# A post-norm attention and int8 FFN layer on one core: rows of the maxima first on SyncE, a wait before stacking queries, and a new table of places

## The reference

```python
q = (x @ Wq) ; k = (x @ Wk) ; v = (x @ Wv)          # heads of 32; k, v shared by 4 query heads
attn = softmax(q @ k.T / sqrt(32)) ; o = (attn @ v) @ Wo
x = layernorm(x + o)
x_scale = max(|x|, axis=2) / 127 ; x_q = round(x / x_scale)
y = (x_q @ w_q.T) * x_scale * w_scale + bias
x = layernorm(x + y)
```

## Time and profile before

| what | value |
|---|---|
| median of 3 runs | 813.49 us (812.19 to 815.58) |
| the profiled execution | 815.75 us, span 813.5 us |
| PE busy | 741.5 us (91%) |
| DVE, POOL, ACT busy | 622.9, 590.9, 479.7 us |
| mean granted TensorE clock | 0.963 |

### The profile page before, as it was taken

The page is one execution under the profiler, slowest core; times in us unless marked ns, Lnnn a source line. Parts: engine busy times, 40 slices in busy tenths (PEclk is TensorE's granted clock), DMA queues, the critical chain, the costliest instruction groups (busy, mean ns, idle before and its releaser), DMA issues.

```text
span 813.5 us, 12175 instructions
## 1 busy us (share of the span) xinstructions
PE 741.5 (91%) x3640; PEld 435.0 (53%) x3640; DVE 622.9 (77%) x1103; ACT 479.7 (59%) x872; POOL 590.9 (73%) x700
## 2 busy tenths in 40 slices
PE   6689989999899989999899998999899998998874
PEld 5355545666366644566446663666446673544431
DVE  5678777778887787877878788877878787888365
ACT  3145556656665565665656566665666566666734
POOL 3208858786987589774988679874988759889825
PEclk9989999999999999999999999999999998999995
DMA  7431313234242323223232332323332342022101
GB/s 216 116 115 43 84 40 95 51 89 110 63 119 59 84 66 118 55 72 99 73 101 68 73 100 64 114 62 89 77 104 56 79 105 72 28 59 73 53 27 52
DMA packets 56431, 65.56 MB, mean 81 GB/s; under 512 B 25664, under 2 KB 27712, under 8 KB 56368
## 3 DMA queue, kind: packets, MB, share of 16 engines
q1 hardware_dynamic: 55296, 62.11, 28.2%
q0 software_dynamic: 1072, 2.69, 1.3%
HBM read 20.71 MB, written 8.39 MB: 36 GB/s over the span
## 4 chain that ended last, share of the span: by engine, by line
PE 61%; DVE 13%; POOL 6%; SPq 5%; issue 5%; ACT 4%; DMA 4%; POOLq 1%; DVEq 0%; ACTq 0%
PE front_bank L325 12%; PE st_bank L379 12%; PE o_bank L397 11%; PE s_bank L370 10%; PE tail_bank L325 7%; DVE row_max L796 6%; POOL prob_sum L1003 5%; PE z_bank L411 4%; SPq L296 3%; DMA q_stack<-neg_max 2%; DMA probs<-in_L_attn_Wv 2%; PE front_bank L332 1%; PE tail_bank L480 1%; SPq L1120 1%; ACT probs L628 1%
## 5 line engine op out<-in xcount | busy, mean ns | idle before, releaser
L628 ACT ACTIVATE probs<-st_bank 128x512 f32<-128x512 f32 x512 | 291.3, 594 | 180.7 <-PE st_bank L379 166.5
L796 DVE TENSOR_REDUCE row_max<-s_bank 128x1 f32<-128x512 f32 x512 | 336.2, 682 | 73.9 <-PE s_bank L370 70.6
L1003 POOL TENSOR_TENSOR prob_sum<-prob_sum,probs 128x512 f32<-128x512 f32 x248 | 311.1, 1286 | 13.4 <-ACT probs L628 13.2
L379 PE MATMUL st_bank<-q_stack,k_stack 98*128 98x512 f32 x512 | 226.4, 444 | 22.6 <-ACT probs L628 12.5
L370 PE MATMUL s_bank<-k_stack,q_stack 96*128 96x512 f32 x512 | 213.7, 419 | 18.0 <-DVE row_max L796 17.1
L1003 POOL TENSOR_TENSOR prob_sum<-probs 128x512 f32<-128x512 f32 x128 | 161.0, 1284 | 50.9 <-PE z_bank L411 27.6
L379 PEld LDWEIGHTS st_bank<-q_stack,k_stack 98*128 98x128 f32 x512 | 98.0, 192 | 122.0 <-ACT probs L628 57.9
L370 PEld LDWEIGHTS s_bank<-k_stack,q_stack 96*128 96x128 f32 x512 | 99.1, 194 | 57.4 <-DVE row_max L796 29.9
L397 PE MATMUL o_bank<-probs,v_tok 128*32 128x512 f32 x1024 | 128.6, 622 | 0.0
L1008 POOL TENSOR_TENSOR rs<-mv,small 128x1 f32<-128x1 f32 x64 | 12.2, 191 | 84.5 <-DVE mv L842 84.3
L397 PEld LDWEIGHTS o_bank<-probs,v_tok 128*32 128x32 f32 x1024 | 27.5, 111 | 62.5 <-issue 56.4
(11 more groups left out here) (186 smaller groups left out, 960.8 us busy)
## 6 DMA issues: line engine op xcount, KB each, us to landing
q_stack<-q_parts SPq DMA_DIRECT2D x357, 64.0 KB, 2.0
x_tok<-in_L_attn_x SPq DMA_DIRECT2D x36, 256.0 KB, 3.3
y_sb<-in_L_attn_x SPq DMA_DIRECT2D x28, 256.0 KB, 2.8
out<-z_sb SPq DMA_DIRECT2D x28, 256.0 KB, 2.2
k_stack<-k_parts SPq DMA_DIRECT2D x90, 64.0 KB, 2.0
probs<-in_L_attn_Wq SPq DMA_DIRECT2D x1, 1024.0 KB, 8.2
prob_sum<-in_L_attn_Wo POOLq DMA_DIRECT2D x4, 256.0 KB, 7.8
q_stack<-neg_max SPq DMA_DIRECT2D x64, 8.0 KB, 1.8
```

The source lines that it names most:

```text
L379: nc.tensor.matmul(st_bank[:, j % 2, :], k_stack[0:STACK_M, p, j, kt * P:(kt + 1) * P], q_stack[0:STACK_M, i, j, :], start=True, stop=True ...
L628: nc.scalar.activation(probs[:, kt, j, :], st_bank[:, j % 2, :], ACT.Exp, scale=SCALE).then_inc(exp_done, 1)
L796: nc.vector.tensor_reduce(row_max[:, i % 2, j * QT + qt:j * QT + qt + 1], s_bank[:, qt % 2, :], AX_X, ALU.max).then_inc(max_done, 1)
L1003: nc.gpsimd.tensor_tensor(prob_sum[:, j, :], first, probs[:, kt, j, :], ALU.add).then_inc(sum_done, 1)
```

## The change

1. `stack_max` is called first in a unit of SP's list instead of after loads, transposing DMAs and stores.
2. Before the 12 DMAs that stack queries of group i for sequence b, SP now waits until the transposed scores of group i of sequence b-1 have been computed (they read the old rows).
3. All pieces of the three tables have new places. Nothing is computed that was not computed before.

```diff
@@ stack_front
                     i = Q_JOB.index(f)
+                    wait(sp, st_done, (b - 1) * UNITS + (i + 1) * QT * NKV)
                     stack_heads(sp, range(NKV), q_stack[:, i, :, :], (hi, hi, lo), q_stacked[i])
@@ segment of SP
                 for u in range(UNITS):
+                    if u in plan["max_lo_dve"]:
+                        i = plan["max_lo_dve"].index(u) + 1
+                        if i < GROUPS or front:
+                            stack_max(b + i // GROUPS, i % GROUPS)
                     for o in range(KC):
...
-                    if u in plan["max_lo_dve"]:
-                        i = plan["max_lo_dve"].index(u) + 1
-                        if i < GROUPS or front:
-                            stack_max(b + i // GROUPS, i % GROUPS)
                     for f, unit in plan["front_dve"].items():
@@ MIDDLE
-    max_lo_dve=(11, 27, 45, 59),
+    max_lo_dve=(11, 25, 45, 59),
-    turn_sp=(15, 26, 41, 46),
+    turn_sp=(22, 29, 41, 46),
-    ffn_pe=(28, 37, 50, 57),
+    ffn_pe=(28, 36, 49, 56),
```

More of the change, by code:

```diff
@@ L45 @@
 MIDDLE = dict(
[L46 to L53, removed]
@@ L54 @@
-    max_pe=(10, 25, 43, 59),
-    max_hi_act=(10, 26, 44, 58),
-    max_lo_dve=(11, 27, 45, 59),
[L57 to L67, removed]
-    turn_sp=(15, 26, 41, 46),
@@ L92 @@
-LAST = dict(
[L93 to L117, removed]
-    ffn_pe=(28, 40, 52, 61),
-    rescale_dve=(28, 39, 49, 58),
-    res2_dve=(29, 39, 50, 58),
-    stats2_dve=(29, 40, 52, 63),
-    rstd2_pool=(33, 45, 53, 60),
-    norm2_act=(33, 45, 57, 63))
+    front_pe={Q3: (0, 1, 2, 4), 0: (5,), 1: (11,), 2: (13,), 3: (17,), K: (20, 22), Q0: (23, 24, 25, 27), V: (29, 30), VT: (32,), Q1: (36, 38), Q2: (44, 45)},
@@ new lines @@
+    front_act={Q3: 3, 0: 5, 1: 10, 2: 14, 3: 17, K: 23, Q0: 26, V: 29, VT: 34, Q1: 38, Q2: 45},
+    front_dve={Q3: 4, 0: 6, 1: 11, 2: 14, 3: 17, K: 22, Q0: 27, Q1: 39, Q2: 45},
+    sums_pe=(5, 18, 39, 54),
+    inv_act=(5, 18, 39, 54),
+    correct_dve=(5, 18, 40, 54),
+    scale_dve=(7, 23, 40, 55),
+    norm_dve=(9, 26, 45, 56),
+    max_pe=(11, 25, 44, 58),
+    max_hi_act=(10, 25, 45, 57),
+    max_lo_dve=(11, 25, 45, 59),
+    o_hi_act=(10, 29, 46, 57),
+    o_lo_dve=(12, 28, 47, 62),
+    wo_pe=((9, 11, 14), (18, 20, 21, 22), (31, 34), (39, 40, 42)),
@@ new lines @@
+    load_sp=(2, 17, 26, 38),
+    res1_dve=(13, 21, 34, 42),
+    stats1_dve=(17, 22, 35, 44),
+    rstd1_pool=(22, 28, 39, 45),
+    norm1_act=(18, 27, 38, 47),
+    maxx_dve=(19, 31, 39, 47),
+    round_act=(20, 31, 39, 47),
+    unround_act=(22, 31, 44, 52),
+    turn_sp=(22, 29, 41, 46),
+    bias_pool=(26, 38, 44, 53),
+    load_x_sp=(1, 1, 2, 6),
+    ffn_pe=(28, 36, 49, 56),
+    rescale_dve=(29, 37, 49, 57),
+    res2_dve=(30, 38, 52, 58),
+    stats2_dve=(32, 38, 53, 61),
+    rstd2_pool=(37, 40, 55, 63),
@@ new lines @@
+    norm2_act=(35, 41, 54, 63))
+FIRST = dict(
+    front_pe={Q3: (3, 4), 0: (8,), 1: (10,), 2: (12,), 3: (14,), K: (17, 19, 20, 21, 22), Q0: (23, 24), V: (28, 30), VT: (32,), Q1: (34, 36, 38, 40), Q2: (44, 46, 50)},
+    front_act={Q3: 5, 0: 8, 1: 10, 2: 12, 3: 14, K: 22, Q0: 24, V: 31, VT: 33, Q1: 40, Q2: 51},
+    front_dve={Q3: 6, 0: 8, 1: 10, 2: 12, 3: 15, K: 21, Q0: 26, Q1: 42, Q2: 51},
+    sums_pe=(13, 23, 34, 52),
+    inv_act=(18, 23, 37, 53),
+    correct_dve=(0, 22, 39, 54),
+    scale_dve=(15, 23, 40, 55),
+    norm_dve=(3, 28, 47, 62),
+    max_pe=(9, 25, 42, 57),
+    max_hi_act=(11, 25, 42, 56),
+    max_lo_dve=(12, 25, 42, 58),
+    o_hi_act=(15, 30, 47, 63),
+    o_lo_dve=(5, 32, 50, 62),
+    load_x_sp=(0, 1, 1, 6))
@@ new lines @@
+LAST = dict(
+    front_pe={Q3: (1, 3, 5, 8)},
+    front_act={Q3: 8},
+    front_dve={Q3: 15},
+    sums_pe=(6, 21, 38, 56),
+    inv_act=(5, 21, 38, 57),
+    correct_dve=(7, 21, 44, 56),
+    scale_dve=(7, 23, 44, 56),
+    norm_dve=(9, 24, 44, 57),
+    max_pe=(10, 26, 45, 60),
+    max_hi_act=(9, 25, 44, 60),
+    max_lo_dve=(13, 29, 47, 60),
+    o_hi_act=(12, 30, 43, 63),
+    o_lo_dve=(12, 33, 45, 61),
+    wo_pe=((10, 13, 14), (19, 24, 25), (31, 32, 35, 36), (42, 43)),
+    load_sp=(4, 16, 33, 39),
+    res1_dve=(14, 25, 37, 45),
+    stats1_dve=(15, 27, 38, 45),
+    rstd1_pool=(18, 31, 41, 47),
+    norm1_act=(18, 31, 39, 47),
+    maxx_dve=(19, 29, 40, 47),
+    round_act=(20, 31, 42, 53),
+    unround_act=(22, 33, 42, 56),
+    turn_sp=(25, 34, 42, 57),
+    bias_pool=(22, 36, 51, 57),
+    load_x_sp=(40, 50, 51, 59),
+    ffn_pe=(27, 38, 53, 61),
+    rescale_dve=(28, 39, 48, 56),
+    res2_dve=(29, 39, 49, 56),
+    stats2_dve=(29, 42, 54, 62),
+    rstd2_pool=(38, 47, 57, 61),
+    norm2_act=(36, 47, 59, 63))
```

21 lines of the change are left out of this document (removed).

## The result

| | before | after |
|---|---|---|
| median, each of 4 runs | 812.89 us | 804.80 us |
| lowest to highest | 812.19 to 815.58 | 804.36 to 805.21 |
| ratio after / before | | 0.9901 [0.9871, 0.9930] |
| profiled execution (span) | 815.75 (813.5) us | 805.21 (803.0) us |

The change is 1.0% faster: 804.8 us where 799.5 was forecast, inside the range of 790 to 811; 8.1 us were won and not 14.0. A later set of runs gave 805.14 us and a ratio of 0.9868 [0.9834, 0.9901]. Before itself varies more than after does: over all sets its runs lie between 807.8 and 819.5 us.

What follows compares the result with a forecast made beforehand. PE was taken as the bound, busy 741.5 of 813.5 us, so only its waits could be won. The terms -9.0 - 4.3 + 3.0 - 1.8 - 1.9 = -14.0 us gave 799.5 us from 813.49, range 790 to 811.

Steps and rivals of the forecast that it cites:

- Units 48 to 52, -9.0 us: Middle segments: moving POOL, ACT and DVE pieces apart cuts PE's idle 1.94 us, 1.5 booked per segment, six times.
- the outer bound of -12.5: Most that units 48 to 52 could win: all 12.5 us of PE's waits for exponentials.
- Unit 32, -4.3 us: Middle segments: the maxima's rows, sent ahead of the transposing DMA, land before unit 32, ending six PE waits, 4.3 us.
- rows of the maxima first in a unit: SP's list: sending these rows first only decides ties, one in MIDDLE (unit 45) and one in LAST; booked 0.
- FFN tile 1 and borrowed units, +3.0 us: Middle segments: a tied transposing DMA for unit 36 and pieces placed before their suppliers cost 0.5 us a segment.
- The new wait, 0: SP before stacking queries: only Q2 waits, for unit 47, and PE's work covers it; 0, at worst 1 us a segment.
- FIRST -1.8: First segment: Q3's matmuls leave the half clock, -1.2 us; a norm leaves its place ahead of four diagonal scalings, -0.6.
- LAST -1.9: Last segment: waits of 1.62 us in unit 40 and 1.26 in 45 shrink, against +0.5 for Q3's later stack.
- The lateness: Rival, chance 0.14: DVE comes out of unit 47 as late as before, the 9.0 us are not won; 811 us.
- Borrowed units: Rival, chance 0.12: four places ahead of their suppliers stall DVE or ACT, costing 21.6 us against 17.0 won; 818 us.
- The clock rival: Rival, chance 0.10: fewer stalls in units 48 to 52 keep full clock, winning six times 1.6 us more; 790 us.
- The signs: Profile values named beforehand for PE's waits, the lengths of middle-segment stretches and SP's queue, to show whether the forecast held.

Runs made afterwards that it cites:

- either row: Two runs on the changed kernel: DVE's o_lo and residual 2 back in unit 49, 811.68 us; ACT's rstd1, x_scale, round and unround back in units 47 and 48, 815.86 us.
- the early half of the table alone: Changed kernel with the new MIDDLE table only for pieces placed before unit 42 and the old one from 42 on: 816.84 us, 1.0034 of before.
- four units more: Changed kernel with SP's new wait before Q2's stack lengthened to the scores of unit 51 instead of 47: 831.78 us, 1.0238 of before.
- both tables old: Both code edits and the new MIDDLE table, with the old FIRST and LAST tables: 804.16 us, 0.9906 of before.
- the three repaired: Changed kernel with tile 2's transposing DMA in unit 45, FFN tile 1 in 37, and rstd1's POOL chain run once before the first segment: 799.87 us, 0.9803 of before.

## Why the prediction was right, and where not

- *Units 48 to 52, -9.0 us.* Right in mechanism, somewhat too small. PE's waits in units 49 to 52 fell from 12.9 to 2.2 us over the six segments, and units 48 to 63 from 129.9 to 117.3, which is the outer bound of -12.5. The segment that was read had 1.94 us of these waits, the six have 2.15 on average; and PE's waits in units 60 to 62, which the sum left out, fell from 7.7 to 4.0. Putting either row back brought the named wait back, on the engine that the forecast named.
- *Unit 32, -4.3 us.* Right for its place: all six waits are gone. But I booked "rows of the maxima first in a unit" as deciding ties alone and looked no further along SP's list. The failed step is that one: it covers the order within a unit, not a queue that is late as a whole. At unit 48 the rows stand behind the stack of Q1, a store and tile 2's transposing DMA of unit 41, a tie that the sum did not work out, and a long stack turns it into a wait. The `unround` of tile 2, which moved from unit 40 to 44, is not what holds that DMA: it was done 1.5 to 2.5 us earlier in every middle segment, and with the early half of the table alone, `unround` back in 40, the same three segments wait 1.15, 1.37 and 1.47 us. So these waits total 8.2 us and not 5. Moving that DMA to unit 45 removed them in the middle segments.
- *FFN tile 1 and borrowed units, +3.0 us.* "A tie, so any late DMA shows" was right, and its share alone was 3.9 us, up to 1.22 in a segment. The borrowed units did not stall PE in five segments. In the second one POOL's pause did it, 1.71 us of wait and a half-clock stretch behind it (from 161.0 us), about 3.5 us in all. The pause stood in the trace of before, under cover of K's matmuls. I had moved K out of unit 20 in the sum without asking what those matmuls hid.
- *The new wait, 0.* Right, and supported from both sides: the code edits alone change nothing that can be told, and four units more cost 3% against the change. The sign named for it, SP free when Q2's stack is released, was wrong. SP was busy with the maxima's rows, and that very lateness is what hides the wait.
- *FIRST -1.8.* The first part failed, the second came otherwise, and in medians no gain is shown. The six matmuls of Q3 were to leave the half clock; they stand in unit 3 now, but half clock at the start lasts 13.7 us instead of 10.2 and covers them there, 0.43 us apart as before (first row below). The wait in unit 47 is gone, not shortened: DVE's four scalings take 1.75 us instead of 3.96. But two steps on the weight shortly before them take 1.02 and 1.38 us instead of 0.50 and 0.43, and PE waits 1.50 us at unit 42 instead. That goes with what POOL does beside them. Before, it adds without a break from 103.91 to 112.66 us, and of the four scalings the first takes 0.27 us and the three others 1.30 to 1.32; after, one takes 1.16 us beside an addition and three 0.28 while POOL stands. It is read from the timelines; no run tried it. After, PE, then DVE and PE:

```profile
48.57 0.63 PE L325 MATMUL front_bank<-x_lo,wq_hi 128*128 128x512 f32 x1
...
103.32 1.38 DVE L891 TENSOR_SCALAR round_sb<-round_sb 128x512 f32<-128x512 f32 x1
109.70 1.75 DVE L896 TENSOR_SCALAR y_sb<-ident,x_scale 128x128 f32<-128x128 f32 x4
...
105.36 0.50 PE L370 MATMUL s_bank<-k_stack,q_stack 96*128 96x512 f32 x1 [1.50 <-DVE row_max L796]
```

  The 1.0 us that FIRST gave is again one pair of profiles: it took 88.9 to 90.9 us in three with the old table and 89.5 to 90.2 in eleven with the new one. Up to 120 us of the span half clock lasts 20.5 or 23.9 us in all eleven, and 13.7, 17.1 and 17.1 in the three.
- *LAST -1.9.* The two waits of the earlier trace rows fell as forecast, the 1.62 us are gone and the 1.26 are 0.60; that the first was a wait for a bank, its row does not say. Against them came 1.19 and 1.66 us for the maxima's rows, which the sum did not have. Over all profiles LAST is near its forecast, with the number against it that is told above (804.16 us with both tables old).
- *The rivals.* The lateness did not move into unit 47. Borrowed units did not make the change slower, though the early half of the table alone is, by 0.3%, in the profile through the clock. The clock rival did not come: between 120 and 770 us as many microseconds at half clock as before, and over the span more. The Trainium skill, "TensorE: Matmul & The Clock Gate", section "What's actually happening", lets the clock follow how busy the array has been recently, and that spoke for this rival. The trace does not bear this use of it out: in the segment of the earlier trace rows PE is now busy 18.14 of 19.20 us of the last quarter and not 18.30 of 21.40, and the clock granted there is 0.91 where it was 0.92. Where stalls grew (the early half alone, the longer wait), the half-clock stretches grew with them.
- *The signs.* Units 48 to 63 under 20.3 us: 19.2. No wait at unit 32: right. Units 0 to 47 within 1 us of 71.4: wrong, 73.2, of which 1.16 is FFN tile 1 and 0.94 the rows of unit 48. Exponentials under 5 us: 6.9, of which 1.7 is the pause. FFN tile 1 under 1 us: wrong in two segments, 1.22 and 1.16.

The sum was -14.0 us and the spans differ by 10.5. Term by term: units 48 to 63 of the middle segments gave 3.6 us more than booked; units 0 to 47 came to +3.0 where -4.3 + 3.0 = -1.3 stood, 4.3 us worse; FIRST was 0.8 worse and LAST, in this profile, 2.8; the start gave 0.8 that nobody booked. Then -14.0 - 3.6 + 4.3 + 0.8 + 2.8 - 0.8 = -10.5. In the medians 8.1 us were won where 14.0 were forecast. The part of this miss that can be named is the 4.3 us of units 0 to 47: FFN tile 1, the pause and unit 48. The rest stays open; FIRST, for which no gain is shown, and the lower granted clock are where to look. The kernel with the three repaired measures 799.87 us, and the forecast had said 799.5; that they meet so closely is luck, since the last quarters gave more than booked and FIRST less.
